# Moving part of the output-projection sum, the row maximum's subtraction and half of the turned copies from VectorE to ScalarE and GpSimd, and loading the attention keys straight from DRAM, in a one-core fused decoder kernel

## The reference

```python
x = _layernorm(x + _L0_attn_ref(x, ...))            # a state-space mixer: 128 heads of 64, 8 groups
x = _layernorm(x + _L0_xattn_ref(x, ctx, ctx, 0, mask))   # cross attention
x = _layernorm(x + _L0_ffn_ref(x, W_gate, W_up, W_down))  # silu(x Wg) * (x Wu), then W_down
```

```python
scores = einsum('bsgrd,btgd->bgrst', xq, xk) / 4 + mask
probs = softmax(scores)
out = einsum('bgrst,btgd->bsgrd', probs, xv)
```

## Time and profile before

| | |
|---|---|
| median of 3 runs | 1633.24 us (1632.52 to 1634.25) |
| the profiled execution, its own time | 1632.91 us |
| its span in the trace | 1631.1 us |
| busy: PE, PEld | 1609.7 us (99%), 1269.6 us (78%) |
| busy: DVE | 1193.6 us (73%) |
| busy: ACT | 946.9 us (58%) |
| busy: POOL | 976.4 us (60%) |

### The profile page before, as it was taken

The page is one execution under the profiler, slowest core; times in us unless marked ns, Lnnn a source line. Parts: engine busy times, 40 slices in busy tenths (PEclk is TensorE's granted clock), DMA queues, the critical chain, the costliest instruction groups (busy, mean ns, idle before and its releaser), DMA issues.

```text
span 1631.1 us, 25632 instructions
## 1 busy us (share of the span) xinstructions
PE 1609.7 (99%) x9124; PEld 1269.6 (78%) x9124; DVE 1193.6 (73%) x2372; ACT 946.9 (58%) x1578; POOL 976.4 (60%) x741
## 2 busy tenths in 40 slices
PE   9999999999999999999999999999999998989998
PEld 7888888888888888888888888888888885544646
DVE  6867587767877686868685868586858789996443
ACT  6756376546745583648373837283728465994231
POOL 4967488657956594749494949395938583331000
PEclk9999999999999999999999999999999999999999
DMA  6332133213412241313231414141403244000000
GB/s 213 136 104 91 46 114 126 78 59 103 128 59 87 90 137 52 98 60 135 78 105 45 137 58 136 46 129 66 136 20 130 91 92 124 2 20 20 14 13 27
DMA packets 73571, 138.85 MB, mean 85 GB/s; under 512 B 6786, under 2 KB 10882, under 8 KB 73092
## 3 DMA queue, kind: packets, MB, share of 16 engines
q1 hardware_dynamic: 73444, 137.21, 26.3%
HBM read 132.98 MB, written 2.63 MB: 83 GB/s over the span
## 4 chain that ended last, share of the span: by engine, by line
PE 93%; DVE 5%; issue 1%; DMA 0%; ACT 0%; SPq 0%; DVEq 0%; ACTq 0%
PE ps_hs L250 8%; PE ps_hs L252 8%; PE ps_hs L251 8%; PE ps_gate L252 8%; PE ps_gate L251 8%; PE ps_gate L250 8%; PE ps_y L1234 7%; PE ps_hs L1242 7%; PE ps_hs L1244 7%; PE ps_hs L1243 7%; PE ps_gate L1218 4%; PE ps_hs L1452 3%; PE ps_dec L1452 3%; PE ps_y L1538 3%; DVE pr L1052 2%
## 5 line engine op out<-in xcount | busy, mean ns | idle before, releaser
L801 DVE SCALAR_TENSOR_TENSOR conv<-ps_hs,cw,conv 128x508 f32<-128x508 f32 (+2 forms) x432 | 320.1, 741 | 31.1 <-ACT conv L568 19.9
L401 POOL TENSOR_TENSOR cum_bc<-cum_bc,neg_cum 128x1024 f32<-128x1024 f32 x128 | 247.6, 1935 | 10.8 <-POOL cum_bc L391 0.3
L250 PE MATMUL ps_hs<-x_hi,w_hi 128*128 128x512 f32 x576 | 231.3, 402 | 0.0
L252 PE MATMUL ps_hs<-x_hi,w_lo 128*128 128x512 f32 x576 | 225.0, 391 | 0.0
L250 PE MATMUL ps_gate<-x_hi,w_hi 128*128 128x512 f32 x576 | 224.3, 389 | 0.0
L251 PE MATMUL ps_hs<-x_lo,w_hi 128*128 128x512 f32 x576 | 224.3, 389 | 0.0
L251 PE MATMUL ps_gate<-x_lo,w_hi 128*128 128x512 f32 x576 | 224.1, 389 | 0.0
L252 PE MATMUL ps_gate<-x_hi,w_lo 128*128 128x512 f32 x576 | 224.1, 389 | 0.0
L1242 PE MATMUL ps_hs<-wo_hi,g_hi 128*128 128x512 f32 x488 | 190.4, 390 | 0.0
L1244 PE MATMUL ps_hs<-wo_hi,g_lo 128*128 128x512 f32 x488 | 189.9, 389 | 0.0
L1243 PE MATMUL ps_hs<-wo_lo,g_hi 128*128 128x512 f32 x488 | 189.8, 389 | 0.0
(11 more groups left out here) (184 smaller groups left out, 3339.2 us busy)
## 6 DMA issues: line engine op xcount, KB each, us to landing
cum_bc<-cum_scratch SPq DMA_DIRECT2D x128, 512.0 KB, 4.1
w_raw<-w_in SPq DMA_DIRECT2D x145, 256.0 KB, 4.7
wo_raw<-w_out SPq DMA_DIRECT2D x64, 256.0 KB, 5.0
g_acc<-x_t SPq DMA_DIRECT2D x4, 512.0 KB, 5.5
acc<-x_nat SPq DMA_DIRECT2D x1, 2048.0 KB, 9.9
out<-y_out SPq DMA_DIRECT2D x8, 256.0 KB, 2.0
wg_sb<-w_gate SPq DMA_DIRECT2D x1, 1792.0 KB, 8.6
wu_sb<-w_up SPq DMA_DIRECT2D x1, 1792.0 KB, 12.6
```

The lines of the kernel that those rows point to most:

```text
L250: eng.matmul(ps, whi, xhi, start=(k == 0), stop=False)
L252: return eng.matmul(ps, wlo, xhi, start=False, stop=(k == n - 1))
L401: gp.tensor_tensor(part, part, start.broadcast_to([P, 2, HB, SEQ]), ALU.add).then_inc(S["bc_ok"], 1)
L801: v.scalar_tensor_tensor(out=dst, in0=src, scalar=cw[:, at, TAPS - 1 - n:TAPS - n], in1=dst, op0=ALU.mult, op1=ALU.add).then_inc(S["tap"], 1)
```

## The change

Six edits, all in the hand-over and the attention loop:

1. `first_part(b)` for b = 2 to 7 leaves VectorE. ScalarE scales `g_acc[:, b, :]` in place by `rstd_g` and GpSimd adds it to `acc` (`add_kept`, signal `acc_gp`).
2. Batch 0 gets its own variance, root, inverse and norm ahead of batch 1's second part.
3. The keys: all eight copies come from DRAM, from an array that the host lays out so that each partition's row is one run of 16 KB; the values are laid out likewise.
4. The maximum of half 1 is subtracted by GpSimd in one instruction of 512 columns (`less_max`, signal `sub_ok`), and ScalarE takes the exponential of half 1 in one instruction of 512 columns instead of four of 128.
5. The turned copy of half 1 alternates: even chunks on VectorE, odd chunks on ScalarE (`keep_turned_too`).
6. The sum `acc += att` goes to GpSimd (`add_attended`). The statistics of a finished batch move one chunk later, and the powers for the second norm are taken in three parts instead of two.

```diff
             for par in range(2):
-                src = ctx_t.rearrange("b (c q d) t -> q d (b c) t", q=2, d=AD)[par]
-                sp.dma_start(k_rep[par * 64:par * 64 + AD, :, :, :].rearrange("p b c t -> p (b c) t"), src)\
-                    .then_inc(S["k_in"], 16)
-            sp.dma_start(v_raw[:, :, :], ctx_nat.rearrange("b t d -> t b d")).then_inc(S["v_in"], 16)
-            sp.wait_ge(S["k_in"], 16 * 2)
-            for par in range(2):
-                first = k_rep[par * 64:par * 64 + AD, :, :, :]
-                for r in range(1, REP):
+                for r in range(REP):
                     p0 = par * 64 + r * AD
-                    sp.dma_start(k_rep[p0:p0 + AD, :, :, :], first).then_inc(S["k_in"], 16)
+                    sp.dma_start(k_rep[p0:p0 + AD, :, :, :].rearrange("p b c t -> p (b c t)"),
+                                 ctx_t[par * AD:(par + 1) * AD, :]).then_inc(S["k_in"], 16)
+            sp.dma_start(v_raw[:, :, :].rearrange("p b d -> p (b d)"), ctx_nat).then_inc(S["v_in"], 16)
...
+            def add_kept(b):
+
+                pool.wait_ge(S["kept_sc"], b - 1)
+                gp.tensor_tensor(acc[:, b, :], acc[:, b, :], g_acc[:, b, :], ALU.add).then_inc(S["acc_gp"], 1)
...
+            for b in range(2, 5):
+                add_kept(b)
+            pool.wait_ge(S["kbd_m"], 3)
+            pool.wait_ge(S["k_in"], 16 * 2 * REP)
+            keys(0)
+            keys(1)
+            for b in range(5, BATCH):
+                add_kept(b)
+            wait_alone(pool, S["v_in"], 16)
...
+            def add_attended(n):
+
+                b, o = n // 2, n % 2
+                pool.wait_ge(S["att_ok"], n + 1)
+                cols = slice(o * 256, (o + 1) * 256)
+                gp.tensor_tensor(acc[:, b, cols], acc[:, b, cols], att[:, o, :], ALU.add).then_inc(S["xa_ok"], 1)
+
+            def less_max(i):
+
+                pool.wait_ge(S["s_max"], 2 * i + 2)
+                part = pr[i % 3][:, REP:2 * REP, :]
+                gp.tensor_tensor(part, part, neg_max[:, i % 3, REP:2 * REP].unsqueeze(2).broadcast_to([P, REP, SEQ]),
+                                 ALU.subtract).then_inc(S["sub_ok"], 1)
...
+                if par:
+                    act.wait_ge(S["sub_ok"], i + 1)
+                    part = pr[i % 3][:, REP:2 * REP, :].rearrange("p r t -> p (r t)")
+                    sc.activation(part, part, ACT.Exp, scale=-1.0).then_inc(S["p_exp"], 1)
+                    return
...
+            def keep_turned_too(i):
+
+                act.wait_ge(S["pt_ps"], 2 * i + 2)
+                need(act, S["pt_v"], i)
+                need(act, S["pv_ps"], 2 * (i - 3) + 2)
+                sc.activation(pr_t[i % 3][:, 1, :], ps_gate[1][:, :], ACT.Copy).then_inc(S["pt_v"], 1)
...
-            root(1, 0, slice(0, 2))
+            act.wait_ge(S["rstd_inv"], GROUPS)
+            act.wait_ge(S["gacc_ok"], BATCH * (2 * GROUPS - 1))
+            for b in range(2, BATCH):
+                sc.activation(g_acc[:, b, :], g_acc[:, b, :], ACT.Copy, scale=rstd_g[:, b:b + 1])\
+                    .then_inc(S["kept_sc"], 1)
+            root(1, 0, slice(0, 1))
             keep_queries(0)
+            root(1, 1, slice(1, 2))
...
+                if i >= 4 and i % 2 == 0:
+                    keep_turned_too(i - 3)
...
-                if i >= 3:
+                if i >= 3 and (i - 3) % 2 == 0:
                     keep_turned(i - 3)
...
+                if i % KD == 3 and i >= 11:
+                    batch_done((i - 11) // KD)
```

More of the change, by code:

```diff
@@ L491, in _, with keys @@
             pool.wait_ge(S["v_ones"], 1)
[L492 to L507 removed]
+            def add_kept(b):
+                pool.wait_ge(S["kept_sc"], b - 1)
+                gp.tensor_tensor(acc[:, b, :], acc[:, b, :], g_acc[:, b, :], ALU.add).then_inc(S["acc_gp"], 1)
+            def keys(i):
                 need(pool, S["s_ps"], 2 * i - 2)
@@ new lines, in powers @@
+            def powers(stage, n, cols):
+                pool.wait_ge(S[f"mv{stage}"], cols.stop)
+                gp.tensor_scalar(rstd[stage - 1][:, cols], mv[stage - 1][:, cols, 1], EPS, None, ALU.add)\
+                    .then_inc(S[f"eps{stage}"], 1)
+                pool.wait_ge(S[f"eps{stage}"], n + 1)
+                gp.tensor_tensor(rstd[stage - 1][:, cols], rstd[stage - 1][:, cols], minus_half[:, cols], ALU.pow)\
+                    .then_inc(S[f"pow{stage}"], 1)
+            def add_attended(n):
[3 more added lines that the diff above has]
+                gp.tensor_tensor(acc[:, b, cols], acc[:, b, cols], att[:, o, :], ALU.add).then_inc(S["xa_ok"], 1)
@@ L513, in _ @@
+            def less_max(i):
[3 more added lines that the diff above has]
+                                 ALU.subtract).then_inc(S["sub_ok"], 1)
+            for i in range(CHUNKS):
+                if i >= 2:
+                    keys(i)
                 if i == 4:
-                    powers(1, slice(2, HB))
+                    powers(1, 0, slice(2, HB))
@@ L515, in _ @@
                 if i == 9:
-                    powers(1, slice(HB, BATCH))
-                if i == 25:
-                    powers(2, slice(0, HB))
-            pool.wait_ge(S["acc_ok"], BATCH * GROUPS)
+                    powers(1, 1, slice(HB, BATCH))
+                if i == 20:
+                    powers(2, 0, slice(0, 2))
+                if i == 27:
+                    powers(2, 1, slice(2, HB))
+                if i >= 2:
+                    less_max(i - 2)
+                if i % 2 == 0 and i >= 10:
+                    add_attended((i - 10) // 2)
@@ L521, in _ @@
+            less_max(CHUNKS - 2)
+            less_max(CHUNKS - 1)
+            for n in range(CHUNKS // 2 - 5, 2 * BATCH):
+                add_attended(n)
+            powers(2, 2, slice(HB, BATCH))
+            pool.wait_ge(S["acc_ok"], BATCH * (GROUPS - 1) + 2)
+            pool.wait_ge(S["acc_gp"], BATCH - 2)
             pool.wait_ge(S["o_ps"], 2 * BATCH * GROUPS)
@@ L1025, in _ @@
             invert_group(GROUPS - 1)
-            for b in range(2):
-                first_part(b)
-                second_part(b)
-                first_stats(b)
-            variances(1, 0, first_two)
-            first_part(2)
-            second_part(2)
-            inverses(1, 0, first_two)
-            normed(1, 0, acc[:, 0, :]).then_inc(S["x1_ok"], 1)
-            for b in range(3, 5):
-                first_part(b)
-                second_part(b)
+            first_part(0)
+            second_part(0)
+            first_stats(0)
+            variances(1, 0, slice(0, 1))
+            first_part(1)
+            inverses(1, 0, slice(0, 1))
+            normed(1, 0, acc[:, 0, :]).then_inc(S["x1_ok"], 1)
+            second_part(1)
+            first_stats(1)
+            variances(1, 1, slice(1, 2))
+            for b in range(2, 5):
+                second_part(b)
+            inverses(1, 1, slice(1, 2))
             normed(1, 1, acc[:, 1, :]).then_inc(S["x1_ok"], 1)
-            first_part(5)
             second_part(5)
-            first_part(6)
             dve.wait_ge(S["m3_neg"], 1)
@@ L1059, in keep_turned @@
                 dve.wait_ge(S["pt_ps"], 2 * i + 2)
+                need(dve, S["pt_v"], i)
                 need(dve, S["pv_ps"], 2 * (i - 3) + 2)
@@ L1072, in attended @@
                                 rec[:, o].broadcast_to([P, REP, REP, AD]), ALU.mult).then_inc(S["att_ok"], 1)
-                dve.wait_ge(S["att_ok"], n + 1)
-                cols = slice(o * 256, (o + 1) * 256)
-                v.tensor_tensor(acc[:, b, cols], acc[:, b, cols], att[:, o, :], ALU.add).then_inc(S["xa_ok"], 1)
             def batch_done(b):
-                attended(b, 1)
                 dve.wait_ge(S["xa_ok"], 2 * b + 2)
@@ L1140, in _ @@
                         attended(BATCH - 1, 0)
+                    if m == 1:
+                        batch_done(BATCH - 2)
                     if m == 2:
+                        attended(BATCH - 1, 1)
+                    if m == 3:
                         batch_done(BATCH - 1)
                     if m == 4:
-                        dve.wait_ge(S["pow2"], 2)
+                        dve.wait_ge(S["pow2"], 3)
                     if m in (4, 5):
```

46 lines of the change are left out of this document (17 added, 29 removed).

## The result

The changed kernel takes 1624.47 us in the median of 6 runs (1623.47 to 1625.02), the kernel before, measured beside it, 1633.01 (6 runs). The ratio is 0.9946, its 95% interval 0.9934 to 0.9959: faster by 0.54%. The forecast was 1624.6. The profiled execution took 1624.73, its span is 1623.0 us.

What follows compares the result with a forecast made beforehand. VectorE and ScalarE were taken to bound the kernel at once. Gains of 1.2 (hand-over), 0.8 (chunks 1 to 7), 3.4 (chunks 8 to 23) and 3.2 (last eight) sum to 8.6 us: 1624.6 us, range 1620.5 to 1630.0.

Steps and rivals of the forecast that it cites:

- The bound: Chunks 8 to 23: VectorE (12.75 us a group of four chunks) and ScalarE (12.69) bound together; relieving one gives almost nothing.
- TensorE's floor of 11.55: Attention loop: TensorE's own work, 11.55 us a group of four chunks, is the next floor and cuts the gain short.
- The estimate of 0.35 for stalls: Loop: 0.35 us a group (0 to 0.8) added to TensorE's 11.55 for two tight places, giving 11.9.
- The tight place that was named: Loop: ScalarE's new copy of half 1 done after 2.1 us, TensorE wanting the bank again after 2.5 us.
- The second place named: Loop: a group of statistics, norm and masks in one run on VectorE; shares the 0.35 us a group for stalls.
- ScalarE's 10.9: Loop: ScalarE's work for a group of four chunks after the change, 10.9 us, the 512-column exponential priced like the copy.
- Chunks 8 to 23: Four groups of the loop, each falling from 12.75 to 11.9 us: a gain of 3.4 us (1.6 to 4.8).
- Hand-over: Before the first turn of queries: TensorE's idle of 1.45 us for VectorE's norm mostly goes, gaining 1.2 us (0.5 to 1.45).
- The remainder of 0.25: Hand-over: the part of TensorE's 1.45 us idle before the first turn of queries that was expected to stay.
- Last eight chunks: Division to last turn before the feed-forward: copies, sums and statistics leave VectorE's chain, gaining 3.2 us (1.5 to 4.5).
- Keys: Key loads: eight loads land by 1356, needed by 1358.9; hidden, worth nothing, costing one for one if later.
- Contention: Rival: the loop's ten norms on VectorE each wait about 1.0 us for GpSimd; 4 us lost, 1628.6 us; chance 0.15.

Runs made afterwards that it cites:

- e1: The changed kernel with the exponentials of half 1 back as before (eight of 128 columns on ScalarE, no subtraction on GpSimd): 1633.39 us, ratio 1.0004.
- e8: The kernel before with only the subtraction of half 1's maximum on GpSimd and its exponential in one instruction: 1637.72 us, ratio 1.0029.
- e10: The kernel before with GpSimd building each masked key twice from chunk 2 on, the other engines' lists unchanged: 1637.90 us, ratio 1.0029.
- e6: The changed kernel with two of four transposes left out in each turn of the probabilities, so half isn't computed: 1620.55 us, ratio 0.9923.
- e7: The changed kernel with the second norm's statistics of a finished batch taken one chunk later still: 1623.90 us, ratio 0.9939.
- e5: The changed kernel with the keys loaded as before, two loads from DRAM and six copies within on-chip memory: 1624.82 us, ratio 0.9947.
- e3: The changed kernel with the sum of the attended values into the running sum back on VectorE: 1628.14 us, ratio 0.9973.

## Why the prediction was right, step by step

- **The bound** (VectorE and ScalarE at once). For ScalarE e1 shows it: with 13.67 us of its own work a group takes 13.67, while VectorE is busy 39.72 of 52.60. For VectorE e8 and e10 show it: ScalarE is relieved in one and unchanged in the other, and in both the groups grow by about what VectorE's sums and norms grow. A kernel in which VectorE is relieved and ScalarE's list stays exactly as before was not run; that it would gain nothing is concluded from e1.
- **TensorE's floor of 11.55, cutting the gain short.** Shown by e6, where only TensorE has less to do and the groups shorten. The estimate of 0.35 for stalls met 0.32 (11.87 - 11.55), but only in part by what it was meant for. The tight place that was named, ScalarE's copy of half 1, costs 0.2 us a group. Another 0.09 belongs to the floor, which left out the longer step from the one turn that scores follow directly. The second place named, statistics and norm in one run, costs nothing in chunks 8 to 23.
- **ScalarE's 10.9.** Too low: e6 holds at 11.25 with ScalarE busy throughout. That is still under TensorE's 11.87, so the error didn't show in the time; the room was 0.6 us a group and not the 1.0 that the forecast reckoned with.
- **Chunks 8 to 23:** 3.4 forecast, 3.45 measured. **Chunks 1 to 7:** 0.8 and 0.90.
- **Hand-over:** 1.2 forecast, 1.60 measured. The remainder of 0.25 didn't stay: TensorE goes into the first turn with no idle. The other 0.15 comes from a turn that follows directly on a product and overlaps it. The root came at 1354.63 (forecast 1354.3), and the norm started at 1355.04 (forecast 1355.2, or 1356.2 if it waits for GpSimd). It didn't start late but was long, 1.32 us instead of 0.55, beside GpSimd's sums, and ended at 1356.36, ahead of the turn at 1356.69.
- **Last eight chunks:** 3.2 forecast, 2.63 measured. This is the term that was sized too high. The wait of 1.66 us did not go but became 0.77. The turns of x2 waited for the division by 1.15, 0.58, 0.56 and 0.71 us before (3.0 in all) and wait by 1.19, nothing, 1.06 and nothing after (2.25): two of the four are gone, and the first and the third are not. Behind both the kernel after has statistics and norms in one run ahead of the division (from 1434.40 and 1448.79), because the statistics moved one chunk later. The forecast counted what this move frees, 0.8 us at the end, and not what it costs ahead of two divisions. e7, which moves the statistics behind the division, takes 1.41 us back.
- **The sum.** The forecast of 8.6 against 8.58 is closer than its terms: the hand-over was 0.40 too low, chunks 1 to 7 0.10 and chunks 8 to 23 0.05, and the last eight 0.57 too high. That these cancel is luck; the terms themselves are right within 0.6 us.
- **Keys:** hidden, as forecast (e5). They were ready by 1353.88, when SyncE's next issue, which waits for them, came, and not at 1356: 8 loads from 1334.57 in at most 19.3 us, 2.4 each.
- **Contention.** In the change as made it costs the norms 0.19 us each (564 to 753 ns), not the rival's 1.0. The sums, which suffer more (425 to 803 ns in e3), had left VectorE with the same change. The Trainium skill (SBUF — State Buffer, on the shared port pair) says that a VectorE instruction with two SBUF inputs, or in a two-port mode, and a GpSimd instruction that reads SBUF shut each other out, and that whichever starts first keeps the pair for its whole length. The traces agree on which instructions suffer: sum 425 to 762 ns (e10), norm 564 to 753, first part 0.75 to 1.59 us, while masks (284 ns) and copies (683 ns), whose data come from PSUM, stay. They don't show the whole length: in e10 the sum ends 0.29 us after GpSimd's row, less than its own 0.43, and by the profile's own note spans on GpSimd are rough. In which mode the norm runs no trace shows.

The edits are not a sum of parts. Taken out one at a time (of edit 6 only the sum) they cost, in medians, 8.9 (exponentials), 4.7 (copies), 3.7 (sum), 3.9 (hand-over) and 0.4 us (keys) above the 1624.47 of the kernel after, over 21 together, against a gain of 8.5.

## What to carry to other kernels

When two engines are the bound together, work must leave both in one change. Here each half measured by itself would have been dropped: with the exponentials left on ScalarE the change gained nothing (e1), and the exponentials' edit alone lost 4.7 us (e8). Before moving work to GpSimd, list what stays on VectorE with both inputs in SBUF: in this kernel such instructions took up to twice as long when they met GpSimd's, and those that read PSUM did not, so the former are the ones to move and the latter the ones to leave. Compare two traces by distances between marks on the engine that bounds the later kernel, not on one that runs ahead.
